# Operand rows at a pitch of 4,352 B, part first, and TensorE's step of attention A in groups of one kind

## The reference

```python
q = heads(x @ Wq + bq)
k = heads(x @ Wk + bk)
val = heads(x @ Wv + bv)
pos = _sinusoid_pos_emb(S, D) @ Wp + bp
content_score = jnp.einsum('bhsp,bhtp->bhst', q + u, k)
pos_score = jnp.einsum('bhsp,htp->bhst', q + v, pos)
pos_score = _relative_shift(pos_score)
score = (content_score + pos_score) / jnp.sqrt(jnp.float32(P))
weights = jax.nn.softmax(score, axis=-1)
out = jnp.einsum('bhst,bhtp->bhsp', weights, val)
```

## Time and profile before

| | |
|---|---|
| median of 3 runs | 10139.81 us (10116.28 to 10143.54) |
| the profiled execution | 10126.49 us, span 10124.7 us |
| TensorE busy | 8878.6 us, 88% of the span |
| VectorE busy | 5925.2 us, 59% |
| ScalarE busy | 5848.2 us, 58% |
| GpSimd busy | 2788.2 us, 28% |
| DMA | 2552.01 MB, mean 252 GB/s |

### The profile page before, as it was taken

The page is one execution under the profiler, slowest core; times in us unless marked ns, Lnnn a source line. Parts: engine busy times, 40 slices in busy tenths (PEclk is TensorE's granted clock), DMA queues, the critical chain, the costliest instruction groups (busy, mean ns, idle before and its releaser), DMA issues. The chain is left out here.

```text
span 10124.7 us, 255387 instructions
## 1 busy us (share of the span) xinstructions
PE 8878.6 (88%) x91488; PEld 5861.3 (58%) x91488; DVE 5925.2 (59%) x12530; ACT 5848.2 (58%) x10811; POOL 2788.2 (28%) x2894
## 2 busy tenths in 40 slices
PE   5888889799788888989978888898997888889899
PEld 3666666445466666644546666664554666666345
DVE  4666664564466666457446666645745666663673
ACT  4766774454476676445447666644545666763454
POOL 2333332100233333210033333321003333332101
PEclk8999999899899999989989999998998999999899
DMA  7999993210699999321079999922107999992210
GB/s 271 404 393 392 406 407 154 67 35 25 259 403 389 388 404 398 142 68 35 24 280 405 394 394 401 395 114 71 32 25 307 402 388 392 406 398 93 66 36 23
DMA packets 439117, 2552.01 MB, mean 252 GB/s; under 512 B 59008, under 2 KB 89216, under 8 KB 175360
## 3 DMA queue, kind: packets, MB, share of 16 engines
q1 hardware_dynamic: 437760, 2534.40, 63.9%
HBM read 1284.53 MB, written 1248.85 MB: 250 GB/s over the span
## 5 line engine op out<-in xcount | busy, mean ns | idle before, releaser
L815 POOL TENSOR_SCALAR z<-z,nmax 128x1024 f32<-128x1024 f32 x2048 | 2277.9, 1123 | 3718.2 <-DVE nmax L764 3718.2
L754 DVE CUSTOM_DVE_ANT_0 z<-sc,z 128x1024 f32<-128x1024 f32 x2048 | 2497.4, 1220 | 1370.1 <-DMA z<-rel_rows 1038.5
L727 ACT ACTIVATE pT<-rg 128x512 f32<-128x512 f32 x4096 | 2449.0, 598 | 715.7 <-PE rg L635 656.1
L635 PE MATMUL rg<-ident,z 128*128 128x128 f32 x16384 | 2523.4, 277 | 58.6 <-issue 51.5
L635 PEld LDWEIGHTS rg<-ident,z 128*128 128x128 f32 x16384 | 1976.5, 142 | 742.3 <-ACT rel L735 296.6
L735 ACT ACTIVATE rel<-rg 128x512 f32<-128x512 f32 x3072 | 1721.9, 596 | 1157.5 <-PE rg L602 638.7
L1065 ACT ACTIVATE pT<-rg 128x512 f32<-128x512 f32 (+3 forms) x2560 | 1226.2, 530 | 830.2 <-PE rg L997 499.9
L602 PE MATMUL rg<-pos_s,qv_s 96*128 96x512 bf16 (+3 forms) x2560 | 908.1, 361 | 614.5 <-DVE rel L789 610.7
L1081 DVE TENSOR_REDUCE mx_b<-sc 128x1 f32<-128x1024 f32 (+7 forms) x1024 | 1004.2, 991 | 527.0 <-PE sc L979 290.0
L656 PE MATMUL op<-pT,xnT 128*32 128x128 f32 x32768 | 1130.2, 279 | 0.0
L656 PEld LDWEIGHTS op<-pT,xnT 128*32 128x32 f32 x32768 | 847.7, 111 | 247.5 <-issue 154.5
(11 more groups left out here) (115 smaller groups left out, 9099.0 us busy)
## 6 DMA issues: line engine op xcount, KB each, us to landing
rel_rows<-rel SPq DMA_DIRECT2D x1024, 1088.0 KB, 8.7
z<-rel_rows SPq DMA_DIRECT2D x1024, 1024.0 KB, 9.2
v_heads<-rel SPq DMA_DIRECT2D x8, 4096.0 KB, 12.6
xnT<-v_heads SPq DMA_DIRECT2D x128, 256.0 KB, 4.4
qu_parts<-z SPq DMA_DIRECT2D x36, 512.0 KB
pos_s<-pos_parts SPq DMA_DIRECT2D x64, 192.0 KB, 9.1
qv_parts<-z SPq DMA_DIRECT2D x24, 512.0 KB
k_parts<-z SPq DMA_DIRECT2D x24, 512.0 KB
```

Source lines behind the costliest of these rows:

```text
L635: mm = e.transpose(rg[:, T_BANK[q], (j - 4 * q) * P:(j - 4 * q + 1) * P], z[:, n % RING, j * P:(j + 1) * P], ident[:, :])
L727: e.activation(pT[:, t % 2, q * CH:(q + 1) * CH], rg[:, T_BANK[q], :], ACT.Exp, scale=SCALE).then_inc(p_ready[q], 1)
L754: e.tensor_tensor_reduce(out=zs, in0=scf[:, 2 * half * CH:2 * (half + 1) * CH], in1=zs, scale=1.0, scalar=-3.0e38, op0=ALU.add, op1=ALU.ma ...
L815: e.tensor_scalar(zs, zs, 1.0, nmax[:, n % 2:n % 2 + 1], ALU.mult, ALU.add).then_inc(AA[done], 1)
```

## The change

It has two parts.

**Layout.** The part tensors become (3 parts, 16 heads, 16 rows, 2,176), so that a row takes 4,352 B, of which 4,096 B are used, and the three parts of a head lie in three separate thirds. The stores and loads are written for this shape. The three stores of a job have the same bytes as before; their target pattern was 8 heads by 16 rows and is now 128 rows at one pitch. The loads keep the same number, order and sizes.

**Order in attention A.** On TensorE a step becomes: rows 3, content 0 | turn 0, turn 1 | content 1, rows 0, tail | turn 2, turn 3, combine, values | rows 1, rows 2. ScalarE takes its copy of chunk 0 between its second and third exp. VectorE copies chunk 3 first, then score 0, the tail, score 1, the maximum, and the product with v. Combine now waits for the tail's copy of the same step.

```diff
-        qu_d = nc.dram_tensor("qu_parts", (H, PARTS * HD, S), BF16).ap()
+        qu_d = nc.dram_tensor("qu_parts", (PARTS, H, HD, LINE), BF16).ap()
...
-                hs = dst[m * (H // KT):(m + 1) * (H // KT), :, :].rearrange("h (a d) s -> a h d s", a=PARTS)
+                hs = dst[:, m * (H // KT):(m + 1) * (H // KT), :, :].rearrange("a h d s -> a (h d) s")
                 for i in range(PARTS):
-                    e.dma_start(hs[i], parts[j % SETS][i]).then_inc(pj_stored[j % SETS], 16)
+                    e.dma_start(hs[i, :, 0:S], parts[j % SETS][i]).then_inc(pj_stored[j % SETS], 16)
...
                 if here(s):
-                    e.wait_ge(tail_copied, base.tiles + (r if here(r - 1) else G))
+                    e.wait_ge(tail_copied, base.tiles + (r + 1 if here(r) else G))
                     combine(p, base, s)
...
-            e.dma_start(q[first:last:2, :], q_src[bass.ds(h, 1), 0:reps * HD, :]
-                        .rearrange("a (r d) s -> (a d) r s", d=HD)).then_inc(done, 16)
+            e.dma_start(q[first:last:2, :], q_src[0:reps, bass.ds(h, 1), :, 0:S]
+                        .rearrange("r a d s -> (a d) r s")).then_inc(done, 16)
...
-            e.dma_start(k[first:last:2, :], k_src[bass.ds(h, 1), i * HD:(i + 1) * HD, :]
-                        .rearrange("a (r d) s -> (a d) r s", d=HD).to_broadcast([HD, reps, S])).then_inc(done, 16)
+            e.dma_start(k[first:last:2, :], k_src[i:i + 1, bass.ds(h, 1), :, 0:S]
+                        .rearrange("r a d s -> (a d) r s").to_broadcast([HD, reps, S])).then_inc(done, 16)
```

More of the change, by code:

```diff
@@ L40 @@
 PARTS = 3
+LINE = S + 128
 SLOTS = 6
@@ L56 @@
 R_ACT = [0, 1, 2]
+R_MID = 0
 R_DVE = 3
@@ L109, in sem @@
             return ctx.enter_context(nc.semaphore(name))
-        qu_d = nc.dram_tensor("qu_parts", (H, PARTS * HD, S), BF16).ap()
-        qv_d = nc.dram_tensor("qv_parts", (H, PARTS * HD, S), BF16).ap()
-        k_d = nc.dram_tensor("k_parts", (H, PARTS * HD, S), BF16).ap()
-        pos_d = nc.dram_tensor("pos_parts", (H, PARTS * HD, S), BF16).ap()
+        qu_d = nc.dram_tensor("qu_parts", (PARTS, H, HD, LINE), BF16).ap()
+        qv_d = nc.dram_tensor("qv_parts", (PARTS, H, HD, LINE), BF16).ap()
+        k_d = nc.dram_tensor("k_parts", (PARTS, H, HD, LINE), BF16).ap()
+        pos_d = nc.dram_tensor("pos_parts", (PARTS, H, HD, LINE), BF16).ap()
         v_d = nc.dram_tensor("v_heads", (H, P, NT * VW), F32).ap()
@@ L663, in step @@
                 began = s >= 0
+                if here(r):
+                    if began or r >= 1:
+                        e.wait_ge(r_copied[0], base.tiles + r)
+                    rows_of(p, base, r, 3)
+                if here(c):
+                    content(p, base, c, 0, not began and c == 0)
                 if here(t):
@@ L670, in step @@
                     turn(t, 0)
-                if here(c):
-                    content(p, base, c, 0, not began and c == 0)
-                if here(t):
                     if here(r - 1):
@@ L678, in step @@
                     turn(t, 1)
+                if here(c):
+                    content(p, base, c, 1, not began and c == 0)
                 if here(r):
-                    if began or r >= 1:
-                        e.wait_ge(r_copied[0], base.tiles + r)
-                    rows_of(p, base, r, 3)
+                    e.wait_ge(r_copied[3], base.tiles + (r + 1))
+                    rows_of(p, base, r, 0)
+                    if here(v - 1):
+                        e.wait_ge(AA["po_copied"], base.tiles + v)
+                    row_tail(base, r, not began and r == 0)
                 if here(t):
@@ L686, in step @@
                     turn(t, 2)
-                if here(c):
-                    content(p, base, c, 1, not began and c == 0)
-                if here(t):
                     e.wait_ge(p_ready[1], base.tiles + (t + 1))
                     turn(t, 3)
-                if here(r):
-                    e.wait_ge(r_copied[3], base.tiles + (r + 1))
-                    rows_of(p, base, r, 0)
                 if here(s):
-                    e.wait_ge(tail_copied, base.tiles + (r if here(r - 1) else G))
+                    e.wait_ge(tail_copied, base.tiles + (r + 1 if here(r) else G))
                     combine(p, base, s)
+                if here(v):
+                    if not here(s):
+                        e.wait_ge(tail_copied, base.tiles + (r + 1))
+                    values(p, base, v)
                 if here(r):
@@ L703, in step @@
                     rows_of(p, base, r, 1)
[L704 to L707, removed]
                     if here(t):
@@ L720, in step, with rows_out, probabilities @@
                 r, t = s + R_LEAD, s + T_LEAD
+                def rows_out(c):
+                    e.wait_ge(r_full[c], base.tiles + (r + 1))
+                    e.activation(rel[:, r % RING, c * CH:(c + 1) * CH], rg[:, R_BANK[c], :],
+                                 ACT.Copy).then_inc(r_copied[c], 1)
+                def probabilities(q):
+                    e.wait_ge(t_full[q], base.tiles + (t + 1))
+                    e.activation(pT[:, t % 2, q * CH:(q + 1) * CH], rg[:, T_BANK[q], :], ACT.Exp,
+                                 scale=SCALE).then_inc(p_ready[q], 1)
                 if here(t):
@@ L724, in step @@
                         e.wait_ge(AA["pv_done"], base.tiles + (t - 1))
[L725 to L728, removed]
+                    probabilities(0)
+                    probabilities(1)
                 if here(r):
@@ L732, in step @@
                         e.wait_ge(rel_out[r % RING], moved(base, r - RING))
+                    rows_out(R_MID)
+                if here(t):
+                    probabilities(2)
+                    probabilities(3)
+                if here(r):
                     for c in R_ACT:
-                        e.wait_ge(r_full[c], base.tiles + (r + 1))
-                        e.activation(rel[:, r % RING, c * CH:(c + 1) * CH], rg[:, R_BANK[c], :],
-                                     ACT.Copy).then_inc(r_copied[c], 1)
+                        if c != R_MID:
+                            rows_out(c)
             in_order(e, b, step)
@@ L781, in step @@
                 first = s < 0 and c < 2
-                if here(c):
-                    score(p, base, c, 0, first)
                 if here(r):
@@ L791, in step @@
                 if here(c):
+                    score(p, base, c, 0, first)
+                if here(r):
+                    e.wait_ge(tail_full, base.tiles + (r + 1))
+                    e.tensor_copy(rel[:, r % RING, S:W], tail).then_inc(tail_copied, 1)
+                if here(c):
                     score(p, base, c, 1, first)
```

3 lines of the change are left out of this document (removed).

## The result

| | before | after |
|---|---|---|
| median | 10138.5 us (10116.3 to 10143.5) | 9984.1 us (9980.3 to 9994.1) |
| ratio to before | | 0.9853, 95% interval 0.9836 to 0.987 |
| span of the profiled execution | 10124.7 us | 9980.1 us |
| TensorE busy | 8878.6 us | 8966.6 us |
| ScalarE busy | 5848.2 us | 5584.6 us |

A forecast was written before the change was run, and what follows sets the result against it. Attention A was taken as bound by DMA bytes and a read-to-score chain together, the projections by half-rate stores. Terms of -100, -50 and -30 sum to -180, forecasting 9960 us, range 9800 to 10070.

The forecast's parts named there:

- Term 1: Projections' stores: 128-row targets use all 16 DMA engines, halving a store's time; -100 us, bounds -80 to -125.
- A projection: End of the projections before attention A: the next phase starts at 138.6, not 150.56; 12 us saved per sequence.
- The 5.4 us: Before attention A: time from the last two jobs' stores ending at 145.2 to SyncE reaching the next phase, kept unchanged.
- B projection: Projections before attention B: stores behind v's end sooner, the phase starts at 1843.3, not 1855.5; 12 us per sequence.
- Positions: Start of the kernel: faster stores of the positions' last job give 4 us.
- The bound of -125: Projections' stores: the largest gain allowed, if SyncE's queue also drains sooner through cheaper store issues.
- Term 2: Operand loads in attention A: the new row pitch speeds reading; -50 us, bounds 0 to -125.
- only the stores gain: Whole kernel: attention A's queue is full and loads are slow for their target; 10040 us, chance 0.27.
- The leftover of 1.95 us a head: Attention A: head time beyond quiet steps and load bytes, as 36.64 MB move at 405 GB/s; all 64 heads -125.
- Term 3: Attention A's new order: a shorter chain saves up to 140 us, but the queue is full; -30 us taken.
- the cap: Attention A: DMA share is already 1.01, so with a shorter chain the read waits longer in the queue.
- a chain of 15.71 us: Attention A: read to score 8.62, to rows 0 1.90, TensorE 5.02, next issue 0.17; three steps, 5.24 each.

The follow-up runs named there:

- pitch_4096: The changed kernel with rows at a pitch of 4,096 B in place of 4,352 B: 9977.0 us, ratio 0.986.
- experiments 3 and 4: The changed kernel at a 4,096 B pitch, 9977.0 us; the kernel before with only its rows lengthened to 4,352 B, 10128.6 us beside 10129.7.

## Why the prediction was right, and where it was not

*Term 1, the stores: right in its mechanism, its size too small, -138 measured against -100.* Stores of parts alone run at a share of 1.02 and 401 GB/s, where I had near 1 and near 385. The working was short in each place:
- *A projection.* It gained 17.5 us, not 12. ScalarE's wait fell by (58.9 - 33.2) / 4 = 6.4, where I had 4.1. From the last parts to the next phase it takes 6.0 us, where I had 4.1 + 5.4 = 9.5. The 5.4 us were the mis-sized piece. I had the last two jobs stored by 145.2 and took what followed as a fixed way out, which the change leaves alone. The kernel before shows bytes moving at half share until 149:

```profile
127.00:128.00 1.00, 0.00 (x0) 0.00 (x0) 0.75 (x1) 1.00 (x3) 0.38 (x1) 0.50 0.46 188
148.00:149.00 1.00, 0.00 (x0) 0.00 (x0) 0.00 (x0) 0.00 (x0) 0.00 (x0) 0.50 0.54 184
149.00:150.00 1.00, 0.00 (x0) 0.00 (x0) 0.00 (x0) 0.00 (x0) 0.00 (x0) 0.50 0.27 107
```

  My sum left out what was still in the queue at 128.87 (at 127 it moves 188 GB/s) and the first operands of q+v, issued behind the last stores. So about 4 of the 5.4 us were transfers, an estimate from these rows, and the faster stores shorten them too. That three stores are now issued in 1.64 us in place of 4.08, which I named for the outer bound, may add to it; no run shows it apart.
- *B projection.* 15 us, not 12, of which 14.3 lie between v's store and the phase.
- *Positions.* 7.5, not 4.

The bound of -125 was too tight by 13.

*Term 2, the loads: the step that failed is "I take -50".* It is 0. The positions' loads alone moved 213 GB/s before, 211 after and 215 in `pitch_4096` (58 to 60 us), and the kernel with either pitch takes the same time. The Trainium skill (DMA: Bandwidth & Descriptors, "Latency and other measured facts") lists 207 GB/s at a row pitch of 512 KiB, less only from 2 MiB on, and no smaller pitch, so experiments 3 and 4 decide here. The rival "only the stores gain" was right on this term and wrong in its time (10040), because term 1 was larger. The leftover of 1.95 us a head was a little high as well: 36.64 MB take 88.9 us at 412 GB/s, which leaves 1.5, since about 0.2 MB of them belong to no tile, operand or v.

*Term 3, the order: the cap was right, the limit that the order removes was not in my sum.* I took -30; 11 to 13 came. I built a chain of 15.71 us in three steps, 5.24 each, from the read issued at 1538.55 to the score at 1547.17, and had the order shorten it by 0.15 us a step. What I left out is the loop inside the step: content 0, score 0, chunk 3, rows 0. It takes 5.21 us at half traffic, where nearly no read is late. The kernel before has, on TensorE and VectorE, behind the content 0 of 1541.00, and for the read issued at 1538.55 its time to landing:

```profile
1546.27 0.60 PE L628 MATMUL sc<-xnT 96*128 96x512 bf16 x2
...
1541.91 1.23 DVE L754 CUSTOM_DVE_ANT_0 z<-sc,z 128x1024 f32<-128x1024 f32 x1 [0.61 <-DMA z<-rel_rows]
...
z<-rel_rows SPq DMA_DIRECT2D x1, 1024.0 KB, 8.4
```

The scores at 1541.91 and 1547.17 start 0.91 and 0.90 us behind their content, the same 0.90 as at half traffic. But the read is no bystander: it lands at 1546.9, 0.2 us ahead of its score, and that is also the distance in the changed kernel, where content 0 comes 1.7 us ahead of the score and only the read can end the wait. So in these quiet steps loop and read end within some hundredths of a microsecond of each other, and the trace can't tell which of them leads. Over all 1,024 first scores of the kernel before, 651 start within 0.24 us of a landing, 416 at the distance from content that half traffic shows (within 0.04 us), and 149 at both; at half traffic these are 10, 932 and 7. My reading that the scores wait for reads was thus right for more than half of them, and the loop is the second limit, which the chain didn't have. The new order removes it whole: 4.90 a step where the queue has room, 0.31 less, not 0.15. My floor "TensorE's own work of 4.95" was nearly right. The cap for which I took only 30 us, the full queue, was right, and stronger than I made it: 11 to 13 us are left of 317. VectorE, kernel after, in quiet steps:

```profile
1535.79 1.23 DVE L770 CUSTOM_DVE_ANT_0 z<-sc,z 128x1024 f32<-128x1024 f32 x1 [0.86 <-DMA z<-rel_rows]
...
1539.50 0.69 DVE L803 COPY rel<-rg 128x512 f32<-128x512 f32 x1 [0.43 <-PE rg L608]
1541.02 1.22 DVE L770 CUSTOM_DVE_ANT_0 z<-sc,z 128x1024 f32<-128x1024 f32 x1 [0.83 <-DMA z<-rel_rows]
```

Here the wait ahead of score 0 is real: the copy of chunk 3 ends 0.83 us before it. Content 0 doesn't end it: it stands at 1539.30, 1.72 us ahead of the score. The step is 5.23, nearly as long as before. The time that the loop gave back has become a wait for memory.

*The signs that I named.* Share of the stores near 1: yes. ScalarE's 58.9 to about 42: it was 33.2. TensorE's 137.2 to about 90: 66.9. GpSimd's 92.2 to about 45: 35.6. A head's GB/s toward 412: no, the heads from 400 to 1500 us move 396 GB/s on the mean after and 400 before. Quiet steps toward 5.1: no. VectorE's waits for reads grow and TensorE's move to combine: both. Turn 1 as a new wait did not show.

*The sum.* The errors offset each other: 38 us too little in term 1, 69 too much in terms 2 and 3. Attention B lost 4, and the medians differ by 10 us more than the two profiled executions. The forecast of 9960 lies 24 us from the measured 9984, closer than its terms deserve, and that is luck.

## What to carry to other kernels

Before costing a queue, look at the share of DMA engines in a stretch where only one kind of transfer runs: 0.51 with every compute engine idle was worth 138 us, and the cure was the shape of one access pattern. Where a wait is put down to a DMA but often ends at the same distance behind another engine's instruction, look for a second limit, and look at when the transfer landed before you acquit it; here both ended together, and a run with half of the traffic parted them. And when two limits lie within a per cent of each other, as here the loop (5.21 us) and the queue (5.25), removing one gives nearly nothing until the other is moved: cut bytes next, as the narrower v did.

## What was unexpected of the hardware

- Issuing a store costs SyncE less when its target is one pattern of 128 rows: three stores of the same bytes take 1.64 us, against 4.08 and 3.80 for 8 by 16 rows. Right behind v's store the difference is small: 6.21 us in the kernel after, 7.05 before.
- The rows of SBUF to which a load goes matter beside other traffic. Loads of the same bytes to adjoining rows took 8.3 us to landing, to every other row 6.6, and cost 113 us over the kernel; alone both moved 211 GB/s.
- A pitch of 4,096 B, a power of two, is as good as 4,352 for these rows: 9977.0 and 9984.1 us.
- Operand loads cost a quarter to almost two fifths more than their bytes: 234 and 260 us for 76.7 MB, in a queue that moves 406 GB/s with tiles alone.
- Two limits can end within hundredths of a microsecond of each other step after step: 149 scores of the kernel before start at the shortest distance from both the read's landing and the content.
